# A wait in the load queue: the query weights and all that follows are requested once the second piece of the inputs has landed

## What is computed

```python
q = _heads(hidden_states @ q_w.T + q_b, b, s)
k = _heads(hidden_states @ k_w.T + k_b, b, s)
v = _heads(hidden_states @ v_w.T + v_b, b, s)
qp = jax.nn.elu(q) + 1.0
kp = jax.nn.elu(k) + 1.0
kv = jnp.einsum('bhsd,bhse->bhde', kp, v)
z = jnp.einsum('bhsd,bhd->bhs', qp, kp.sum(axis=2))[..., None]
attn = jnp.einsum('bhsd,bhde->bhse', qp, kv) / (z + EPS)
out = attn.transpose(0, 2, 1, 3).reshape(b, s, HID)
return out @ o_w.T + o_b
...
x = _layernorm(x + _L0_attn_ref(...), axis=-1)
```

## Time and profile before

| | us |
|---|---|
| median of 3 runs (lowest, highest) | 432.15 (432.05, 432.84) |
| the profiled execution | 431.72 |
| its span | 429.8 |

### The profile page before, as it was taken

How to read it: one execution, slowest core, us unless ns; L and a number is a source line. 1 busy time by engine, 2 the same in 40 slices (tenths; PEclk the granted TensorE clock), 3 DMA queues, 4 the chain that set the end, 5 groups by cost and what they waited for, 6 DMA issues and landing times.

```text
span 429.8 us, 9350 instructions
## 1 busy us (share of the span) xinstructions
PE 414.1 (96%) x3645; PEld 361.1 (84%) x3645; DVE 262.8 (61%) x637; ACT 241.8 (56%) x423; POOL 275.8 (64%) x237
## 2 busy tenths in 40 slices
PE   8999999999999999899999999999799999999993
PEld 6888999988889888788888899798588989888882
DVE  4678657748536348966663588646465776555463
ACT  4757653764484775452743767573537757453633
POOL 1644454564898677575876548457658387787863
PEclk9999999999999999999999999999999999999998
DMA  7644000021233313042222103122523332554402
GB/s 245 206 144 150 3 2 0 2 74 51 73 82 129 98 61 124 24 127 96 76 88 76 38 2 110 55 83 63 173 86 98 105 103 70 162 159 148 139 33 98
DMA packets 19623, 39.29 MB, mean 91 GB/s; under 512 B 2763, under 2 KB 7371, under 8 KB 19580
## 3 DMA queue, kind: packets, MB, share of 16 engines
q1 hardware_dynamic: 19004, 38.17, 28.9%
q10 hardware_dynamic: 576, 0.53, 0.4%
HBM read 37.08 MB, written 1.08 MB: 89 GB/s over the span
## 4 chain that ended last, share of the span: by engine, by line
PE 79%; DVE 11%; issue 3%; ACT 3%; DMA 1%; POOL 1%; SPq 0%; DVEq 0%; POOLq 0%; ACTq 0%
PE bank L487 13%; PE bank L488 13%; PE bank L490 13%; PE bank L755 8%; PE bank L757 8%; PE bank L756 8%; PE bank L835 2%; PE bank L774 2%; PE bank L823 1%; DVE hraw L1617 1%; DVE sil L1601 1%; DMA q_buf<-x_cols_dram 1%; PE bank L510 1%; PE bank L805 1%; PE bank L806 1%
## 5 line engine op out<-in xcount | busy, mean ns | idle before, releaser
L1299 POOL TENSOR_TENSOR h_lo<-hraw,h_hi 128x512 fp32r<-128x512 f32 x76 | 99.7, 1315 | 77.2 <-ACT h_hi L1089 77.2
L487 PE MATMUL bank<-xT_hi,pk_hi 128*128 128x512 f32 x256 | 102.9, 402 | 1.1 <-DVE hraw L1617 1.1
L488 PE MATMUL bank<-xT_hi,pk_lo 128*128 128x512 f32 x256 | 101.0, 394 | 0.0
L1089 ACT ACTIVATE h_hi<-hraw 128x512 fp32r<-128x512 f32 x76 | 47.8, 629 | 77.9 <-DVE hraw L1617 76.0
L1617 DVE TENSOR_TENSOR hraw<-bank,sil 128x512 f32<-128x512 f32 x76 | 52.4, 689 | 51.8 <-ACT sil L1077 24.5
L490 PE MATMUL bank<-xT_lo,pk_hi 128*128 128x512 f32 x256 | 80.4, 395 | 0.0
L755 PE MATMUL bank<-pk_hi,h_hi 128*128 128x256 f32 x272 | 77.8, 286 | 1.3 <-POOL h_lo L1299 1.0
L1305 POOL TENSOR_TENSOR pk_lo<-pk_raw,pk_hi 128x512 fp32r<-128x512 f32 (+1 forms) x44 | 75.1, 1706 | 2.7 <-ACT pk_hi L1107 2.6
L757 PE MATMUL bank<-pk_hi,h_lo 128*128 128x256 f32 x272 | 76.8, 282 | 0.0
L756 PE MATMUL bank<-pk_lo,h_hi 128*128 128x256 f32 x272 | 76.8, 282 | 0.0
L487 PEld LDWEIGHTS bank<-xT_hi,pk_hi 128*128 128x128 f32 x256 | 48.2, 188 | 11.8 <-DVE hraw L1617 1.6
(11 more groups left out here) (255 smaller groups left out, 730.7 us busy)
## 6 DMA issues: line engine op xcount, KB each, us to landing
pk_raw<-pk_f_dram SPq DMA_DIRECT2D x28, 384.0 KB, 3.3
pk_raw<-pk_f_dram SPq DMA_DIRECT2D x16, 512.0 KB, 3.4
pk_raw<-pk_f_dram SPq DMA_DIRECT2D x16, 256.0 KB, 3.0
kv_buf<-pk_x_dram SPq DMA_DIRECT2D x4, 512.0 KB, 3.5
x_tok<-x_rows_dram SPq DMA_DIRECT2D x1, 1024.0 KB, 9.1
pk_raw<-pk_x_dram SPq DMA_DIRECT2D x4, 256.0 KB, 5.9
brow<-cw_dram SPq DMA_DIRECT2D x4, 256.0 KB, 3.2
cw_late<-cw_dram SPq DMA_DIRECT2D x4, 256.0 KB, 3.6
```

The source lines that it names most:

```text
L487: pe.matmul(o, w(kc)[0], x(kc)[0], start=kc == 0, stop=False)
L488: pe.matmul(o, w(kc)[1], x(kc)[0], start=False, stop=False)
L1089: A(h_hi[:, row, at * 512:(at + 1) * 512], hraw[:, s % 2, :], ACT.Copy).then_inc(sems["hid_hi"], 1)
L1299: pool.tensor_tensor(h_lo[:, row, q], hraw[:, s % 2, :], h_hi[:, row, q].bitcast(F32), ALU.subtract).then_inc(sems["hid_lo"], 1)
```

## The change

SP waits, between the issues of lines 362 and 363, until the second piece (line 361, in_xT0) has landed. Nothing else differs; in the changed kernel all lines from 363 on have a number higher by one.

```diff
             sp.dma_start(q_buf[:, 0, S:2 * S], xc[:, 0, S:2 * S]).then_inc(sems["in_xT0"], 16)
             sp.dma_start(q_buf[:, 1, 0:512], xc[:, 1, 0:512]).then_inc(sems["in_xT1"], 16)
+            sp.wait_ge(sems["in_xT0"], 16)
             sp.dma_start(wa_raw[:, :, 0:D], w_attn0[:, :, 0:D]).then_inc(sems["in_w0_q"], 16)
             sp.dma_start(q_buf[:, :, 512:1024], xc[:, :, 512:1024]).then_inc(sems["in_xT2"], 16)
```

## The result

| | kernel before | with the wait |
|---|---|---|
| median of 15 runs each, taken together | 432.56 us (431.08 to 435.25) | 434.50 us (432.39 to 437.37) |
| ratio to before, 95% interval | | 1.0060 (1.0038 to 1.0081) |
| the profiled execution, and its span | 431.72, 429.8 us | 432.39, 430.5 us |

The ratio means 2.6 us slower (0.006 x 432.56), with an interval from 1.6 to 3.5 us, in which the 1.9 us between the two medians lie too. The forecast was 432.8 us, no change to be seen, and the range ended at 433.8: it was wrong, and on the side of rival 1. Lines from 363 on stand one further down in this kernel.

What follows compares the result with a forecast made beforehand. Bound: TensorE's chain (79%), its start hanging on SP's loads. bo 1.2 us later less 0.58 slack starts line 625 0.62 later, swallowing the 0.55 gained; 0.65 carried gives median 432.8 us from 432.15, range 430.7 to 433.8.

Steps and rivals of the forecast that it cites:

- rival 1: At the second piece and the refill: piece lands at 7.06 as now, refill takes 1.6 us; +1.4, 433.5 us; chance 0.28.
- Term 1: At SP's added wait: it ends at 6.5 us, and TensorE's first part gains up to 0.55 us.
- Term 2: SP's queue behind the wait: full rate from 7.9 us, then 366 GB/s; bo lands at 15.8, 1.2 us later.
- rival 3: At the second piece: without SP's continued issues it lands near 4.8 us; -1.1, 431.0 us; chance 0.18.
- Term 3: Who waits for the loads: only bo lacks cover; through GpSimd's adds and the mask, line 625 starts 0.62 us later.
- Rival 2: At VectorE's query adds: both run in a row after GpSimd's first add; -0.55, 431.6 us; chance 0.18.
- I carry 0.65 to the end: From line 625 to the gate matmul at 40.70: no slack, so 0.65 us of delay is carried to the end.

Runs made afterwards that it cites:

- e3: The changed kernel with only GpSimd's second bias add moved behind the remainders of the expert packs; ratio to the kernel before 1.0008 (0.9987 to 1.0029).
- e12: The changed kernel with the wait two loads later, behind the second half of the inputs; ratio to the kernel before 1.0022 (0.9998 to 1.0046).
- e13: The changed kernel repeated unchanged, beside one with eight matmuls of zeros; ratio to the kernel before 1.0073 (1.0034 to 1.0111).
- e5: The kernel before, unchanged, measured against itself; ratio 0.9984 (0.9952 to 1.0016).
- e15: The kernel before, without the wait, with eight matmuls of zeros added ahead of the attend; ratio to the kernel before 0.9991 (0.9957 to 1.0025).
- e7: The changed kernel with the wait one load later, behind the load of the query weights; ratio to the kernel before 1.0011 (0.9981 to 1.0041).
- e2: The changed kernel with both of GpSimd's bias adds moved behind the remainders of the expert packs; ratio to the kernel before 1.0053 (1.0026 to 1.0080).
- e8: The changed kernel waiting for line 362's load (second channel chunk) instead of the second piece; ratio to the kernel before 1.0081 (1.0052 to 1.0110).
- e1: The changed kernel repeated unchanged; ratio to the kernel before 1.0068 (1.0036 to 1.0100).
- e16: The changed kernel repeated unchanged once more, beside one with eight matmuls of zeros; ratio to the kernel before 1.0059 (1.0028 to 1.0089).

## Why the prediction was wrong, point by point

- **Where and how** was right: the wait blocks, the queue empties for 1.5 us, bo loses its cover, VectorE's query adds stand behind GpSimd's bias adds, the mask releases attend late, and attend's lateness reaches the gate undiminished. e3 shows it by taking one link away.
- **Term 1** was on the cautious side: SP goes on at 6.21, 5.95, 6.40 and 6.34 us in the four profiles, where 6.5 was taken. The second piece took 4.3 to 4.7 us, where 5.4 was measured before.
- **Term 2 failed.** "Full rate from 7.9" and "afterwards, at 366 GB/s" put bo at 15.8; it landed at 17.0, although the wait ended 0.3 us early. By its own formula from 6.2 the landing is 15.5, so the refill was mis-sized by 1.5 us. Of that 1.2 us are in the windows: against 366 GB/s from 7.6 on, 94 KB are missing from 7.5 to 8.5, 191 in the next us, 126 in the next and 35 in the last half, 446 KB. I had seen such a weak stretch in before at 3 to 5 us, named it in rival 3, and put it down to issues that crowd a transfer, not to what follows each restart. Why the rate is weak there stays open.
- **Term 3**: S at 17.16 instead of 15.92 (+1.24), attend at S + 6.21 instead of S + 6.46 (-0.25): 22.4 becomes 23.4, measured 23.37. The first key eviction came at 14.36 (13.2 taken) and the second query eviction ended at 19.33 (18.6), both by Term 2 again. That they had cover held only because GpSimd was late too; in e12 VectorE's readiness decides.
- **Rival 1** decides "from a bo landing after 16.0 on", and that came true, by the refill and not by the wait's end at 7.06. Its 433.5 was nearest.
- **Rival 2** did not occur as written. In the change the first query add alone got in between the two bias adds (the second of them, which takes 2.39 us alone in e3, takes 2.82 from 19.50 on), and the second query add stood behind it. A form of the rival did occur: in e13, the same kernel, bo came so late (17.8) that the first query add was issued first; attend was at 21.41, earlier than in before. What decides is who issues first. The Trainium skill, "SBUF — State Buffer", section "Who interferes with whom", says as much, that the later issuer waits for the whole of the other; here the trace agrees, with 0.69 us for a query add issued first and 2.17 and 2.33 us for the one issued behind a bias add (e12, e13).
- **Rival 3** did not occur, but a part of its mechanism did. From 4 to 5 us the rate is 304 to 351 GB/s in the four profiles of the change, against 225 and 257 in before and e5: without the issues behind it the second piece does run faster. From 3 to 4 us it is as weak as before (148 to 192 against 169 and 160), and so the piece lands at 5.95 to 6.4 and not near 4.8.
- **"I carry 0.65 to the end"** is the second failure. The gate shift is 1.6, 1.1, -0.3 and 1.65 us in the four profiles of the change, 1.0 on average; the four ratios mean 2.6, 2.9, 3.2 and 2.6 us. So 1 us of the loss at least, and by the averages 1.8, arises behind 42 us, as far as four profiles stand for all runs. That it is the clock behind TensorE's pause isn't shown: the filler that would mend this gains in the control e15 too, the three profiles of the change with a pause of over 2 us have the clock at 1.00 there, and the mean clock of the runs leaves room for 0.5 us. It is of the size by which the stages behind differ from one profile to another (386.8 to 391.8 us), and which kernel gets how much of that stays **open**. I had written that I was wrong if the difference arose behind 41 us; in part it does.
- The Trainium skill, "DMA: Bandwidth & Descriptors", section "Rules for kernel authors", says to issue early and wait late. The runs agree in direction: the wait costs 0.6%, and one load later (e7) 0.1%, not to be told from nothing. The 2.0 us of fixed cost that the prediction took from the same page of the Trainium skill is there the set-up and the completion of a transfer together, fitted to loads that GpSimd issues. Beside the 1.4 us of the refill alone it was not like for like, and what was missing here lay in the rate behind the restart.

## What to carry to other kernels

When a wait is put into a load queue, count the time in which the queue is empty and the weak rate that followed each restart here for 2 to 3 us, and then look for the first consumer without cover. Where VectorE and GpSimd both add SBUF operands, write down which of the two will issue first, since a shift of 1 us in either can turn the order round: in two executions of the changed kernel the attend started at 23.37 and at 21.41. Give every experiment that seems to prove a cause its control in the kernel before: eight matmuls of zeros "repaired" the change, and behind 42 us they won about half as much in a kernel with nothing to repair.

## What the runs showed that I had not expected

- The transfer rate after a restart: in the change 235, 175, 240 and 296 GB/s from 7.5 to 11 us, then 356; in e12, whose queue never ran dry, 281 and 223 GB/s in the stretch after 365.
- A cast of 128x8 numbers, 0.15 us alone, took 2.31 us beside GpSimd's adds (e2). It waits as a large add does.
- Behind a pause of 2.78 us TensorE kept the clock of 1.00 for 1.3 us more and then ran at 0.50 for 3.2 us (e8); behind pauses of 2.10, 2.45 and 2.37 us (e1, the change, e16) it stayed at 1.00 in the profiles.
- With eight added matmuls at 21 us two kernels were faster behind 42 us, one without any use for them (e15: 0.9991 with attend 1.1 us late; its interval reaches to no gain at all). Why was not found.
